# A decoder layer with attention, lag attention and routed experts: half of the last rows on VectorE, lags marked by one replacement, stores and loads on two queues, and a first expert slot with one item

## The reference

```
mean_value = corr.mean(axis=(1, 2))
_, index = jax.lax.top_k(mean_value.mean(axis=0), TOP_K)
weights = mean_value[:, index]
tmp_corr = jax.nn.softmax(weights, axis=-1)
```

## Time and profile before

| what | value |
|---|---|
| median of three runs | 726.97 us |
| time of the profiled execution | 724.67 us |
| its span | 722.6 us |
| TensorE (PE) busy | 597.1 us, 83% |
| VectorE (DVE) busy | 528.8 us, 73% |
| GpSimd (POOL) busy | 421.7 us, 58% |
| ScalarE (ACT) busy | 411.7 us, 57% |
| mean granted clock of TensorE | 0.91 |

### The profile page before, as it was taken

How to read it: one execution, slowest core, us unless ns; L and a number is a source line. 1 busy time by engine, 2 the same in 40 slices (tenths; PEclk the granted TensorE clock), 3 DMA queues, 4 the chain that set the end, 5 groups by cost and what they waited for, 6 DMA issues and landing times.

```text
span 722.6 us, 15623 instructions
## 1 busy us (share of the span) xinstructions
PE 597.1 (83%) x3724; PEld 470.6 (65%) x3725; DVE 528.8 (73%) x1628; ACT 411.7 (57%) x1194; POOL 421.7 (58%) x446
## 2 busy tenths in 40 slices
PE   4999999999999976679873598898987888887884
PEld 1555555555655544578772398887877877887774
DVE  5799999999999995458778734566656656656664
ACT  3657778867877744177650232365555555645653
POOL 3999899989989921165530254525554554454452
PEclk9999999999999995589865688999999999999997
DMA  5501111111511045175525011101111111111110
GB/s 157 175 1 30 30 31 29 29 45 52 76 29 29 29 84 110 54 207 170 145 47 107 17 38 41 39 17 39 38 35 34 34 37 34 33 37 34 30 39 23
DMA packets 51027, 40.96 MB, mean 57 GB/s; under 512 B 21987, under 2 KB 41318, under 8 KB 50982
## 3 DMA queue, kind: packets, MB, share of 16 engines
q1 hardware_dynamic: 45990, 29.88, 16.5%
q0 software_dynamic: 4992, 10.56, 5.6%
HBM read 27.54 MB, written 12.88 MB: 56 GB/s over the span
## 4 chain that ended last, share of the span: by engine, by line
PE 55%; DVE 14%; ACT 12%; issue 8%; another core or an unknown queue 4%; DMA 3%; POOL 2%; ACTq 1%; SPq 0%; DVEq 0%; POOLq 0%
PE bank L1285 49%; PE bank L1289 4%; ACT xh L666 3%; DVE hid L1277 1%; DVE on L908 1%; ACT nb_c L663 1%; ACT ex L642 1%; ACT shared L786 1%; PE bank L1493 1%; DVE st_e L855 1%; DVE R L869 1%; DVE X L1119 1%; ACT rl L643 1%; DMA ct<-in_ctx_r 1%
## 5 line engine op out<-in xcount | busy, mean ns | idle before, releaser
L539 POOL TENSOR_TENSOR shared<-v,qk 128x1152 f32<-128x1152 f32 x64 | 142.7, 2230 | 2.8
L1285 PE MATMUL bank<-shared,tri_s 128*128 128x360 f32 (+1 forms) x384 | 136.2, 491 | 0.8 <-DVE R L869 0.8
L604 POOL DMA_INDIRECT shared<-xs_d,row_u x92 | 89.1, 968 | 81.1 <-DVE row_u L1188 36.5
L611 POOL DMA_INDIRECT out_x<-shared x64 | 63.4, 990 | 110.2 <-DVE shared L1258 79.2
L1277 DVE TENSOR_TENSOR hid<-bank,shared 128x256 f32<-128x256 f32 x156 | 64.1, 423 | 60.7 <-ACT shared L786 34.5
L786 ACT ACTIVATE shared<-bank 128x256 f32<-128x256 f32 x156 | 59.1, 383 | 80.3 <-PE bank L1285 50.7
L869 DVE TENSOR_TENSOR R<-bank,qk 128x360 f32<-128x360 f32 (+1 forms) x192 | 96.2, 541 | 7.3 <-PE bank L1285 5.4
L1285 PEld LDWEIGHTS bank<-shared,tri_s 128*128 128x128 f32 x384 | 69.5, 192 | 44.8 <-issue 20.3
L1285 PE MATMUL bank<-w_s,hid 128*128 (+1 forms) x624 | 90.5, 289 | 5.2 <-issue 3.5
L1285 PE MATMUL bank<-shared,ct 128*128 128x128 f32 x512 | 73.0, 287 | 21.5 <-DVE hid L1277 14.1
L1285 PEld LDWEIGHTS bank<-w_s,hid 128*128 128x128 f32 x624 | 82.8, 205 | 7.3 <-issue 6.0
(11 more groups left out here) (243 smaller groups left out, 1153.1 us busy)
## 6 DMA issues: line engine op xcount, KB each, us to landing
xs_d<-xs SPq DMA_DIRECT2D x16, 270.0 KB, 4.4
X<-in_x SPq DMA_DIRECT2D x16, 256.0 KB, 2.7
ct<-in_ctx_t SPq DMA_DIRECT2D x16, 256.0 KB, 2.9
ct<-in_ctx_r SPq DMA_DIRECT2D x16, 256.0 KB, 3.6
gram_d<-gd SPq DMA_DIRECT2D x14, 256.0 KB, 2.4
circ<-prob_d SPq DMA_DIRECT2D x32, 64.0 KB, 2.9
w_s<-in_w_up SPq DMA_DIRECT2D x4, 512.0 KB, 4.8
shared<-xs_d,row_u POOLq DMA_INDIRECT x92
```

What stands on the lines that cost most here:

```text
L539: nc.gpsimd.tensor_tensor(outer[k], v9[k % 2][:].unsqueeze(3).broadcast_to([P, H, D1, D]), kk.unsqueeze(2).broadcast_to([P, H, D1, D]), AL ...
L604: nc.gpsimd.indirect_dma_start(xg[q], None, xs_d[:, :], bass.IndirectOffsetOnAxis(ap=rows, axis=0)).then_inc(xg_in[q], 16)
L611: nc.gpsimd.indirect_dma_start(out[:, :], bass.IndirectOffsetOnAxis(ap=xg[(NXI + j) % NX][:, DEST:DEST + 1].bitcast(U32), axis=0), yg[q], ...
L1285: return nc.tensor.matmul(o, l, r, start=start, stop=stop, skip_group_check=True)
```

## The change

- The last group's rows 2 and 3 (`last_rows`) move from ScalarE to VectorE: a product `last_mr`, a bias, two rows. They stand on VectorE ahead of the sum `mean_early`. ScalarE keeps rows 0 and 1.
- The second half of the last gram store is issued by ScalarE, right behind its own write of `gd`; the first half stays on SP.
- The lags are marked by one replacement: the last three of the eight maxima are overwritten with -3e38, and `match_replace` writes the scores with the five maxima replaced by 3e38 into `keep`; `away` then is -1e30 wherever `keep` is below 3e38. Index search, cast, comparisons and their sum are gone.
- For groups 0 and 1 the second half of circ is loaded by ScalarE, between its fourth and fifth copy of value products.
- The first expert slot holds item 1 alone: item 0's gather, transpose, four up products, silu, product, down products and accumulation are gone. In the first two slots in which there is a pair before, TensorE turns the next rows after that pair's up products, not ahead of them (`late_rows`).

The diff, cut to its core (left out are the declarations, two constants, and VectorE's part of the expert slot, in which the same `items_of` replaces `range(2)`):

```diff
             if i is None:
                 return (j, m - XS, m % NX, m // NX) if -XS <= j < NT else None
             return UNROLL * i + j, UNROLL * i + m - XS, m % NX, UNROLL // NX * i + m // NX
+
+        def items_of(i, j):
+
+            return (1,) if i is None and j == -XS else (0, 1)
 
         def new_pair(j):
 
...
                 sp.wait_ge(d_gd, g + 1)
-                for h in range(2):
+                for h in range(2 if g < NG - 1 else 1):
                     first_b = (g - DIAG_PARTS[-1][1]) * 2 * GT + h
                     sp.dma_start(bass.AP(gram_t.tensor, first_b * PITCH, [[2 * L, L], [2 * PITCH, GT], [1, 2 * L]]),
                                  gd[g % 2][h * L:(h + 1) * L].rearrange("p t a b -> p t (a b)")).then_inc(gram_out[g % 2], 16)
...
             def circ_load(g, p, r):
 
-                for h in range(2):
+                for h in range(2 if g >= 2 else 1):
                     src = bass.AP(prob_d.tensor, g * (GT * 2 * 2 * L) + (h * 2 * L + 1), [[1, L], [2 * 2 * L, GT], [1, L]])
                     sp.dma_start(circ[p][h * L:(h + 1) * L, :, h * L:(h + 1) * L], src).then_inc(circ_in[p], 16)
...
-            for m in range(NXI):
+            for m in range(1, NXI):
                 gather(m)
...
-            def norm(g, p, rs, rs_sem, mr, mr_sem, nb, nb_sem, dst, dst_sem):
+            def norm(g, p, rs, rs_sem, mr, mr_sem, nb, nb_sem, dst, dst_sem, own=GT):
...
-                for k in range(GT):
+                for k in range(own):
...
-                for k in range(GT):
+                for k in range(own):
...
-                    norm(g, p, rs_c, c_rs, mr_c, c_mr, nb_c, c_nb, xh2, d_xh)
+                    norm(g, p, rs_c, c_rs, mr_c, c_mr, nb_c, c_nb, xh2, d_xh, GT // 2 if i is None and g == NG - 1 else GT)
...
+            act.wait_ge(d_gd, NG)
+            first_b = (NG - 1 - DIAG_PARTS[-1][1]) * 2 * GT + 1
+            act.dma_start(bass.AP(gram_t.tensor, first_b * PITCH, [[2 * L, L], [2 * PITCH, GT], [1, 2 * L]]),
+                          gd[(NG - 1) % 2][L:2 * L].rearrange("p t a b -> p t (a b)")).then_inc(gram_out[(NG - 1) % 2], 16)
...
-            for g in range(EARLY_V, PRE):
+            for g in range(EARLY_V, PRE - 1):
                 copy_u(g)
+            act.wait_ge(prob_out, 16)
+            act.wait_ge(circ_0, 2)
+            for g in range(2):
+                src = bass.AP(prob_d.tensor, g * (GT * 2 * 2 * L) + (2 * L + 1), [[1, L], [2 * 2 * L, GT], [1, L]])
+                act.dma_start(circ[g][L:2 * L, :, L:2 * L], src).then_inc(circ_in[g], 16)
+            copy_u(PRE - 1)
...
-                    wide = (1 + new) * P
-                    nc.scalar.activation(xgT[p][:, 0:wide], bank[0][:, 0:wide], ACT.Copy, scale=scale_s[:, 0:1]).then_inc(x_xT, 1)
+                    cols = slice(items_of(i, j)[0] * P if new else 0, (1 + new) * P)
+                    nc.scalar.activation(xgT[p][:, cols], bank[0][:, cols], ACT.Copy, scale=scale_s[:, 0:1]).then_inc(x_xT, 1)
...
-                    if up:
+                    if up and h in items_of(i, up[0]):
...
+            def last_rows(g, p):
+                half = slice(GT // 2, GT)
+                dve.wait_ge(c_mr, g + 1)
+                dve.wait_ge(c_rs, g + 1)
+                nc.vector.tensor_tensor(last_mr[:], mr_c[:, half], rs_c[p][:, half], ALU.mult).then_inc(last_nb, 1)
+                dve.wait_ge(last_nb, 1)
+                nc.vector.tensor_scalar(nb_c[p][:, half], last_mr[:], 1.0, None, ALU.add).then_inc(last_nb, 1)
+                dve.wait_ge(last_nb, 2)
+                dve.wait_ge(d_tr, g)
+                for k in range(GT // 2, GT):
+                    nc.vector.tensor_scalar(xh2[:, k, :], X[:, GT * g + k, :], rs_c[p][:, k:k + 1], nb_c[p][:, k:k + 1],
+                                            ALU.mult, ALU.add).then_inc(d_xh, 1)
+
+            last_rows(NG - 1, (NG - 1) % 2)
...
             mean_step(nc.vector.max(top8[:], bank[4][:, 0:L]))
-            mean_step(nc.vector.max_index(top_at[:], top8[:], bank[4][:, 0:L]))
-            mean_step(nc.vector.tensor_copy(top_f[:], top_at[:]))
-            mean_step(nc.vector.tensor_tensor(kept_k, iota_s[:, 0:L].unsqueeze(1).broadcast_to([P, LAGS, L]),
-                                              top_f[:, 0:LAGS].unsqueeze(2).broadcast_to([P, LAGS, L]), ALU.is_equal))
-            mean_step(nc.vector.tensor_reduce(keep[:], kept_k.rearrange("p k l -> p l k"), AX.X, ALU.add))
+            mean_step(nc.vector.memset(top8[:, LAGS:8], -3e38))
+            mean_step(nc.vector.match_replace(keep[:], top8[:], bank[4][:, 0:L], 3e38))
             dve.wait_ge(mean_mm, 2)
             mean_step(nc.vector.tensor_tensor(mean[:], bank[3][:, 0:L], mean_early[:], ALU.add), False)
-            mean_step(nc.vector.tensor_scalar(away[:], keep[:], 1.0, 1e30, ALU.subtract, ALU.mult))
+            mean_step(nc.vector.tensor_scalar(away[:], keep[:], 3e38, -1e30, ALU.is_lt, ALU.mult))
...
+            def turn_rows(i, tr):
+                j, t, q, r = tr
+                new = i is None and j < 0
+                need(pe, x_xT, t)
+                for h, (qq, rr) in enumerate(new_pair(j) if new else [(q, r)]):
+                    if not new or h in items_of(i, j):
+                        pe.wait_ge(xg_in[qq], 16 * rr + (16 if qq > 0 else 0))
+                        last = nc.tensor.transpose(bank[0][:, h * P:(h + 1) * P], xg[qq][:, 0:E], id_s[:])
+                last.then_inc(x_tr, 1)
...
-                if tr:
-                    j, t, q, r = tr
-                    new = i is None and j < 0
-                    need(pe, x_xT, t)
-                    for h, (qq, rr) in enumerate(new_pair(j) if new else [(q, r)]):
-                        pe.wait_ge(xg_in[qq], 16 * rr + 16)
-                        last = nc.tensor.transpose(bank[0][:, h * P:(h + 1) * P], xg[qq][:, 0:E], id_s[:])
-                    last.then_inc(x_tr, 1)
+                late_rows = i is None and n < 1 - XS
+                if tr and not late_rows:
+                    turn_rows(i, tr)
...
-                    for h in range(2):
+                    for h in items_of(i, j):
...
-                        last.then_inc(x_up, 1)
+                        last.then_inc(x_up, 2 // len(items_of(i, j)))
+                if tr and late_rows:
+                    turn_rows(i, tr)
...
-                    for h in range(2):
+                    for h in items_of(i, j):
```

More of the change, by code:

```diff
@@ L148, in build @@
         xh2 = sb("xh2", [P, GT, E])
+        last_mr = sb("last_mr", [P, GT // 2])
         x2T, k2T = sb("x2T", [P, GW]), sb("k2T", [P, GW])
@@ L154, in build @@
         mean, mean_early, mean_late = (sb(n, [P, L]) for n in ("mean", "mean_early", "mean_late"))
-        top8, top_at, top_f = sb("top8", [P, 8]), sb("top_at", [P, 8], U32), sb("top_f", [P, 8])
+        top8 = sb("top8", [P, 8])
         keep, away, scores = sb("keep", [P, L]), sb("away", [P, L]), sb("scores", [P, L])
@@ L265, in build @@
         gram_out = sems("gram_out", 2)
+        last_nb = sem("last_nb")
         diag_in, mean_ch, mean_mm, prob_e = sem("diag_in"), sem("mean_ch"), sem("mean_mm"), sem("prob_e")
@@ L785, in expert_slot @@
                         need(act, x_h, 2 * t - 3 + h)
-                        nc.scalar.activation(silu[p][h], bank[1 + 2 * p + h][:, HID:2 * HID], ACT.Silu).then_inc(x_silu, 1)
+                        nc.scalar.activation(silu[p][h], bank[1 + 2 * p + h][:, HID:2 * HID], ACT.Silu
+                                             ).then_inc(x_silu, 2 // len(items_of(i, up[0])))
                     if h == 0 and xt and (i is not None or xt[0] >= 0):
@@ L1232, in expert_slot @@
                             acc = X[:, dyn(at, 1), :].rearrange("p a e -> p (a e)")
-                            if h == 0:
+                            if h == items_of(i, j)[0]:
                                 dve.wait_ge(x_dn, t + 1)
                                 dve.wait_ge(x_gt, t + 1)
-                            need(dve, x_acc, k)
+                                need(dve, x_acc, 2 * (j + XS))
+                            else:
+                                dve.wait_ge(x_acc, k)
                             nc.vector.scalar_tensor_tensor(acc, bank[6 + p][:, h * P:(h + 1) * P], gate[:, h:h + 1], acc,
-                                                           ALU.mult, ALU.add).then_inc(x_acc, 1)
+                                                           ALU.mult, ALU.add).then_inc(x_acc, 2 // len(items_of(i, j)))
                         dve.wait_ge(x_acc, 2 * (j + XS) + 2)
@@ L1269, in expert_slot @@
                         nc.vector.scalar_tensor_tensor(eq[p][:, h, :], row[:, EXPERT:EXPERT + TOPK], item,
-                                                       row[:, GATE:GATE + TOPK], ALU.is_equal, ALU.mult).then_inc(x_eq, 1)
+                                                       row[:, GATE:GATE + TOPK], ALU.is_equal, ALU.mult
+                                                       ).then_inc(x_eq, 2 // len(items_of(i, j)))
```

(10 more changed lines are left out.)

1 line of the change is left out of this document (removed).

## The result

The changed kernel's median is 717.65 us (four runs, 714.25 to 721.57), beside 727.97 us for the kernel before on the same chip. The ratio is 0.9857, with a 95% interval of 0.981 to 0.9905: 10.3 us less, between 6.9 and 13.8. I had forecast 722.0 in a range of 717.5 to 726, that is 5.0 us less. The direction was right, the time lay at the edge of the range, and the gain was about twice the forecast.

What follows compares the result with a forecast made beforehand. The bound was taken as the chain of waits, at the barrier and the experts' start. Terms 1.24 + 0.62 + 1.1 + 2.0 = 5.0 us off the 726.97 median gave 722.0, range 717.5 to 726.

Steps and rivals of the forecast that it cites:

- A: At the barrier, half of the last rows on VectorE: 1.24 us gained, between 0.6 and 1.24.
- B: At the barrier, the last gram store issued from two queues: 0.62 us of issue time gained, low end 0.
- C: At the barrier, lags marked by one replacement, 0.53 for 1.8: gain 1.27; with the circ loads 1.1 arrives, ends 0.66 and 1.9.
- D: Second circ loads issued by ScalarE: 1.1 us together with the lag marking, ends 0.66 and 1.9.
- Rival 3: At the barrier, next link late: rows 0.6, gram store 0, probabilities behind the context load 0.66; 723.7 us, chance 0.16.
- the forecast's own sign: Forecast wrong if circ's products start less than 2 or more than 4 us earlier from rs_c.
- E: At the experts' start, the first slot with one item: 2.0 us gained, low end 0, high end 2.9.
- rival 1: In the cross stage, the granted clock stays up: 2.5 us more gained, 719.5 us, chance 0.17.
- The replay: Experts' start replayed from the first transpose at 411.96: fourth slot's transposes 9.0 after it instead of 11.2, about 2.0 earlier.
- rival 4: Experts' earlier start paid back at the first hold-up at 420.77: first-slot gain 0, 724.0 us, chance 0.12.
- the order is the old one again: At the fourth expert slot, the old order resumes and its transposes, at 423.13 before, start about 2.0 us earlier.
- Rival 2: Among the straight-line expert slots, a third hold-up costs 6.7 us: 728.7 us, slower than before, chance 0.07.

Runs made afterwards that it cites:

- e1: The changed kernel with the first slot's parts undone, leaving the barrier's parts alone; 718.05 us, ratio 0.9933 to the kernel before.
- e2: The kernel before with the first slot's parts alone, the barrier as it was; 713.56 us, ratio 0.9898 to the kernel before.
- p3: The whole changed kernel, with SP loading the 64 sorted tiles in plain order; 653.19 us, ratio 0.9106 to the kernel before.
- p1: The barrier's parts alone, with SP loading the 64 sorted tiles in plain order; 656.72 us, ratio 0.9147 to the kernel before.

## Why the prediction came out as it did

**A, 1.24 forecast.** From rs_c's start to the end of the last gd: 6.8 to 7.3 without A, 7.05 on average of four traces, 5.2 to 6.2 with it, 5.92 of ten: 1.13. VectorE's rows cost 0.30 each, less than the 0.38 taken. mean_early ended at 284.44, well ahead of the late load, so the cover held.

**B, 0.62 forecast.** It gave 0.15. The two issues went out together as said; the step that failed was that a later issue is a later landing. My low end of 0 was the nearer one.

**C and D, 1.1 forecast.** C itself was sized well: from the end of the eight maxima (288.96) to mean 0.49, against my 0.53. But from mean_late's end to the circ products the traces give 10.04 before and 9.38 after, 0.65: the low end of 0.66, and its reason, that the store stays behind the context load, came true. Only the mechanism behind it is another one, as the fifth context load on ScalarE's queue showed. Rival 3 had this step right.

**The barrier together.** Circ products 24.67 after rs_c's start without A to D (four traces), 22.72 with all of them (nine): 1.95, not the 2.96 forecast, and not the 2.76 of the first pair of traces. By the forecast's own sign, less than 2 from rs_c, that is just a miss. Timed alone it came to 4.8, with 1.9 to 7.9 as its interval (and with plain loads to 4.7 without E, 0.6 with it), so the timed runs can't say which. The clock of rival 1 did come along in places: the first circ group took 1.13 instead of 2.05 in the changed kernel, but 2.04 again in e1, and 1.24 in e2, which has none of A to D, so it isn't a gain of the change. From the circ products to TensorE's product of select and R the traces differ from 103.4 to 112.0, in kernels whose code there is the same, 106.2 on average without A to D and 106.5 with them. The difference of 2.7 in that stretch in the first pair (106.8 and 104.1) says nothing.

**E, 2.0 forecast.** This is the term that was mis-sized where E stands alone: 7.4 and 7.6 by timed runs. Behind A to D it came to 3.5 (p3 under p1), from which 2.0 can't be told. The replay was right as far as it went: it had the fourth slot ready at 9.0 after the first transpose, and the chain shows TensorE running dry at 415.26, 8.84 after it. Then a late count paid the start back, as rival 4 said, and at the fourth slot nothing was left: over the traces 11.0 after the first transpose with E (ten), 10.1 without it (four). The failing step is the sentence that the order is the old one again there, so that later slots keep their pace. From the fourth slot's transposes to the first sorted tile's, traces with E take 33.8 to 41.9, 37.6 on average, and those without it 39.0 to 45.5, 41.6 on average. TensorE stands idle in that stretch for 2.6 with E and 5.2 without it, on average, and the chains' hold-ups sum to 5.8 and 9.7; but single traces overlap widely (0 to 11.3 with E, 1.5 to 20.5 without it). I had read the two gaps of the earlier trace rows as fixed. They differ from trace to trace, and on average E has fewer. That they depend on how GpSimd's gathers fall against TensorE's slots is my reading; the gather-first kernel, which loses 10 us in the loop by an order and a wait alone, speaks for it, but why an odd first item should give the better phase was not tried and stays open.

**The total.** The direction was right, but that 717.65 lies in the range is luck: its low end, 717.5, was kept for the clock and for B to D at their high ends, and none of these came. By the traces A to D and E come to 1.95 + 3.0 = 5.0, the forecast's own sum with other terms in it: B and C with D smaller, E won at another place than the one replayed. The first pair of traces alone is no account of it: its 8.7 us are 2.8 in the barrier, 2.7 in the unchanged cross stage and sort, 0.7 in the item slots and 2.5 behind them, where kernels with the same code scatter as much. What the timed 10.3 has beyond 5.0 is not located.

Rival 2, a third hold-up that makes it slower, did not come at its price: the straight item slots have two again, of 2.92 and 2.90, and the wait of 2.18 is a short one of the same kind.

## What to carry to other kernels

When a chain has gaps that no recorded release explains, find out what they depend on before costing anything ahead of them: here they cost some 58 us (719.64 against 661.38), six times what the edit gained, and their number differs from trace to trace. Let a term sum end only where the following work is known to keep its pace. And price a store that goes out earlier by its landing: a transfer in flight took back most of what two of the three moved issues had gained.

## What the runs showed of the hardware

With one gather and one write per slot on GpSimd (0.97 and 0.99 us), the last 55 loop slots took 205 to 220 us; with only one of them on GpSimd, 153.4 to 153.6, with TensorE busy throughout the window of 480 to 640 us. In the first case, and in the item slots with two gathers each, TensorE's counts arrive late, by 4.4 us at the first hold-up of the kernel before (products that ended at 421.51, counted at 425.94); with one transfer a slot none in the loop was more than 0.8 late. ScalarE's and VectorE's counts are on time in both. The path on which they are held isn't shown; SP's plain transfers also read or write rows in order, and that was not separated from their leaving GpSimd.

The granted clock stood at 0.50, the lower of its two levels (1.2 GHz), for 10.2 us at the experts' start in the changed kernel, so E's earlier products ran at it: 2.08 for 8 records at 407.34, where 16 records take 1.95 at 2.4 GHz, as at 422.25.

```profile
404.70:414.90 10.20, 7.93 (x33) 6.96 (x34) 3.15 (x16) 2.51 (x4) 7.59 (x9) 0.50 0.27 55
```
